# Order of the DMA issues for the score stacks in a Flamingo block on one core: k, then q, then the shift rows, and the low part of q on another engine

## The chip, the cores and the metric

The kernel runs on one core of one Trainium2 chip. The metric is the device time of one execution, in microseconds (us), from first to last instruction with what lies around it. A profiled execution gives a span, first to last instruction of the program, and a time of its own that is slightly longer.

## The reference

Input x is 32 batches of 256 rows by 256 columns in f32, and a context of the same shape. The block is gated cross attention followed by a gated feed-forward network with fake quantisation:

```python
# attention: 16 heads of 16, rotary tables on q and k, band |i-j| <= 50
q = rope(layernorm(x) @ Wq.T + bq)
k = rope(ctx @ Wk.T + bk)
v = ctx @ Wv.T + bv
p = softmax(where(band, q @ k.T / 4, -1e9))
x = x + tanh(g_xattn) * ((p @ v) @ Wo.T + bo)
# feed-forward: weights to 4 bits in blocks of 32, activations to 16 bits
h = act_qdq(layernorm(x))
up, gate = act_qdq(h @ qdq(w_up).T), act_qdq(h @ qdq(w_gate).T)
g = act_qdq(gate * qdq16(sigmoid(gate)))
x = x + tanh(g_ffn) * (act_qdq(g * up) @ qdq(w_down).T)
```

## The kernel before

The program has three stages: the weights are prepared (to about 50 us), attention runs over the 32 batches (to about 840 us), and the feed-forward stage follows. The change touches the attention stage alone.

Attention is a software pipeline written out by hand. Each engine has one instruction queue and runs the same loop `steps(rnd, unit)`, one round per batch, cut into eight slots. In the round of batch b0 the engines also work on the batches before it: b1 is one round older, b2 two, b3 three, b4 four; `nxt` is one younger. Synchronisation is by semaphores, so an engine that waits for one value holds up everything behind it on its queue. TensorE is PE, VectorE is DVE, ScalarE is ACT, GpSimd is POOL, SyncE is SP. SP issues every DMA.

The scores need more precision than bf16 gives, so q and k are each split into three bf16 parts. For n in q, k: POOL adds the two products of the rotation (`rotate`), ACT rounds it to the high part (`high`), DVE subtracts (`remainder`), ACT rounds the rest to the middle part (`middle`), and one more subtraction makes the low part (`low`). For k, `low` is on DVE at the head of slot 5. For q, it is on POOL at the end of slot 5, after that slot's `cut`. SP then stores the parts to DRAM (`store_parts`, 384 KB) and loads them back into a stack of 96 rows, `k_stack` or `q_stack`, in three DMAs of 384, 256 and 128 KB (`load_stacks`). The load waits until the store has landed. There are three buffers of each stack.

PE multiplies the stacks twice. `scores` (L835, S_FIRST = 11: pair 0 of batch b1 in slot 3, a round after its parts were made) gives q by k; PE waits there for both stacks. DVE takes the row maxima out of it (`maxima`, L707). The negated maxima are the shift: DVE splits them (`shift_parts`, L720 and L722), PE transposes them, ACT copies them to `shiftT` (L608), and SP writes them in four small DMAs as rows 96 and 97 of `q_stack` (`load_shift`, L471), half 0 for heads 0 to 7 and half 1 for heads 8 to 15. `scoresT` (L852, ST_FIRST = 18: pair 0 of batch b2 in slot 2) gives k by q with the shift inside the product, and waits on the shift rows of that half. ACT takes exponents of it (L596), POOL cuts the band (L527, L536), and PE weighs V (L878).

In one round SP goes through: shift rows half 0 of b2, load of the q stack of b1, x and context of the next batch, the store and the reload for the residual, shift rows half 1 of b2, store of k of b0, store of q of b0, load of the k stack of b0. Its round begins, in time, when the engines are at slots 0 and 1 of theirs.

Of the kernel before, what the change touches and what calls it, by code (L numbers as in the profile page):

```python
# [12 lines left out]
ALU = mybir.AluOpType  # L13
# [60 lines left out]
def reached(eng, sem, batch, per, k):  # L74

    value = batch.n * per + k
    if value <= 0:
        return
    eng.wait_ge(sem, value)
# [229 lines left out]
def attention(nc, dram, x, ctx_in, scratch, banks, keep):  # L309

    with ExitStack() as ctx:
# [95 lines left out]

            return (slot - first) % SLOTS, (first + (slot - first) % SLOTS) // SLOTS

        def low(eng, by, b, n):  # L410

            if not b.real:
                return
            reached(eng, mid_ready[n], b, 1, 1)
            by.tensor_tensor(parts[n][:, 2, :], rest[n][:], parts[n][:, 1, :], ALU.subtract)\
                .then_inc(low_ready[n], 1)

        S_FIRST, ST_FIRST, PV_FIRST = 11, 18, 20
        block = ctx.enter_context(nc.Block())

        @block.sync
        def _(sp):
            def load_x(b):
                if not b.real:
                    return

                reached(sp, x_transposed, b.before(1), 1, 1)
                sp.dma_start(x_in[:], rows_x[b.n]).then_inc(x_loaded, 16)
                reached(sp, c_transposed, b.before(1), 1, 1)
                sp.dma_start(c_in[:], rows_c[b.n]).then_inc(c_loaded, 16)  # L430

            def load_residual(b):
                if not b.real:
                    return

                bb = b.before(NBUF)
                if bb.n >= 0:
                    sp.wait_ge(x2_stored[b.buf], bb.rnd * 16 + 16)
                reached(sp, x2_normed, bb, T, T)
                sp.dma_start(x2[b.buf][:], rows_x[b.n]).then_inc(xres_loaded[b.buf], 16)  # L440

            def store_parts(b, n):
                if not b.real:
                    return

                reached(sp, mid_ready[n], b, 1, 1)
                reached(sp, low_ready[n], b, 1, 1)

                if b.n >= NBUF:
                    sp.wait_ge(stack_loaded[n][b.buf], b.rnd * 48)  # L450
                sp.dma_start(scratch[n][b.buf].rearrange("k (a d) (h t) -> (d h) (k a) t", a=2, h=H),
                             parts[n][:].rearrange("p k (a t) -> p (k a) t", a=2)).then_inc(parts_stored[n], 16)

            def load_stacks(b, n):
                if not b.real:
                    return
                stack = (q_stack if n == "q" else k_stack)[b.buf]
                reached(sp, parts_stored[n], b, 16, 16)
                reached(sp, scoredT, b.before(NBUF), 2 * PAIRS, 2 * PAIRS)
                row = 0  # L460
                for g in range(3):
                    rows = (3 - g) * DK
                    sp.dma_start(stack[row:row + rows, :, :].rearrange("r s t -> r (s t)"), scratch[n + "_rows"](b.buf, g)).then_inc(stack_loaded[n][b.buf], 16)
                    row += rows

            def load_shift(b, half):
                if not b.real:
                    return
                reached(sp, shiftT_copied, b, HALVES, half + 1)
                for k in range(SHIFT):  # L470
                    sp.dma_start(q_stack[b.buf][STACK + k:STACK + k + 1, half * 8:half * 8 + 8, :],  # L471
                                 shiftT[half][k * 8:(k + 1) * 8, :]).then_inc(shift_loaded[half][b.buf], 16)

            def store_x2(b):
                if not b.real:
                    return
                reached(sp, x2_ready, b, 1, 1)
                sp.dma_start(scratch["x2"][b.n], x2[b.buf][:]).then_inc(x2_stored[b.buf], 16)

            def steps(rnd, unit):  # L480
                load_shift(Batch(rnd, unit, 2), 0)
                load_stacks(Batch(rnd, unit, 1), "q")
                load_x(Batch(rnd, unit, -1))
                store_x2(Batch(rnd, unit, 4))
                load_residual(Batch(rnd, unit, 3))
                load_shift(Batch(rnd, unit, 2), 1)
                store_parts(Batch(rnd, unit, 0), "k")
                store_parts(Batch(rnd, unit, 0), "q")
                load_stacks(Batch(rnd, unit, 0), "k")

            run(steps)
            for k in range(NBUF):
                sp.wait_ge(x2_stored[k], 16 * len(range(k, B, NBUF)))

        @block.gpsimd
        def _(pool):
# [43 lines left out]
            def steps(rnd, unit):  # L540
                for slot in range(SLOTS):
                    if slot == 5:
                        scale_of(Batch(rnd, unit, -1), moments_taken, scale_steps, scale_ready, moments, scale_small, scale)
                    if slot == 2:
                        rotate(Batch(rnd, unit, 0), "k")
                    if slot == 3:
                        rotate(Batch(rnd, unit, 0), "q")
                    if slot == 1:
                        scale_of(Batch(rnd, unit, 4), moments2_taken, scale2_steps, scale2_ready, moments2, scale2_small, scale2)
                    pair, late = pair_at(slot, ST_FIRST)  # L550
                    cut(Batch(rnd, unit, late), pair)
                    if slot == 5:
                        low(pool, nc.gpsimd, Batch(rnd, unit, 0), "q")

            run(steps)
            nc.gpsimd.partition_all_reduce(keep["peak"][:, 6:7], keep["lnconst"][:, 0:1], P, RMAX).then_inc(pool_ready, 1)
# [105 lines left out]
        def _(dve):  # L662
# [27 lines left out]
            def remainder(b, n):  # L690
                if not b.real:
                    return
                reached(dve, high_ready[n], b, 1, 1)

                nc.vector.tensor_tensor(rest[n][:], rot[n][:], parts[n][:, 0, :], ALU.subtract)\
                    .then_inc(rest_ready[n], 1)

            def maxima(b, pair):
# [3 lines left out]
                for t in range(T):  # L702
# [6 lines left out]
                            scale=1.0, scalar=-3e38, op0=ALU.add, op1=ALU.max, accum_out=smax[b.buf][:, t, h:h + 1])  # L709
                    ins.then_inc(max_taken, 1)  # L710

            def shift_parts(b, half):

                if not b.real:
                    return
                reached(dve, max_taken, b, 2 * PAIRS, PAIRS * (half + 1))

                reached(dve, shift_transposed, b.before(1), HALVES, half + 1)
                src = smax[b.buf][:, :, half * 8:half * 8 + 8]
                nc.vector.tensor_copy(shift[:, :, half, 0, :], src).then_inc(shift_high, 1)  # L720
                reached(dve, shift_high, b, HALVES, half + 1)
                nc.vector.tensor_tensor(shift[:, :, half, 1, :], src, shift[:, :, half, 0, :], ALU.subtract)\  # L722
                    .then_inc(shift_ready, 1)
# [31 lines left out]
            def steps(rnd, unit):  # L755
                nxt, b0, b1, b2, b3, b4 = (Batch(rnd, unit, k) for k in range(-1, 5))
                for slot in range(SLOTS):
                    if slot == 0:
                        residual(b4)
                    if slot == 1 and 0 <= b0.n < NBUF:  # L760

                        nc.vector.memset(k_stack[b0.n][STACK:P, :, :], 1.0).then_inc(ones_rows_set, 1)
                    if slot == 2:
                        rope(b0, "k", bank_b)
                        divide(b3, 0)
                    if slot == 3:
                        shift_parts(b2, 1)
                        rope(b0, "q", bank_a)
                    if slot == 4:
                        remainder(b0, "k")  # L770
                    if slot == 5:
                        low(dve, nc.vector, b0, "k")
                        remainder(b0, "q")
                    if slot == 7:
                        shift_parts(b1, 0)
                    pair, late = pair_at(slot, S_FIRST)
                    maxima(Batch(rnd, unit, late), pair)
                    if slot == 5:
                        divide(b3, 1)
                    if slot == 4 and nxt.real:  # L780
                        reached(dve, x_loaded, nxt, 16, 16)
                        statistics(nxt, x_in, stats, moments, stats_taken, moments_taken)
                    if slot == 7 and b4.real:
                        reached(dve, xn2T_copied, b4, 1, 1)
                        nc.vector.tensor_reduce(keep["xmax"][:, b4.n:b4.n + 1], keep["xnT"][:, :, b4.n * S:(b4.n + 1) * S],
                                                XY, ALU.max, apply_absolute_value=True).then_inc(xmax_taken, 1)
# [934 lines left out]
```

## Time and profile before

| | |
|---|---|
| Runs | 1406.34, 1407.23, 1412.29 us, median 1407.23 |
| Profiled execution, its own time | 1405.53 us |
| Its span | 1403.8 us |
| Mean granted TensorE clock | 0.941 |
| Busy over the span | PE 85%, DVE 86%, ACT 60%, POOL 42% |
| DMA queue of SP | 132,250 packets, 205.86 MB |

Busy shares are averages over three stages. What the change touches must be read inside the attention stage, in one round and from the waits there.

### The profile page before, as it was taken

To read this page: it belongs to the slowest core of one execution; us is meant where nothing else is said; L and a number is where in the kernel's file an instruction comes from. 1 tells how busy PE (TensorE), PEld (TensorE's weight loads), DVE (VectorE), ACT (ScalarE), POOL (GpSimd) and SP (SyncE) were. 2 spreads that over 40 slices of the span, in tenths; PEclk is the share of its full clock that TensorE was granted. 3 is DMA by queue.
4 is the path that set the end of the run, shared out by engine and by line. 5 is a ranking of instruction groups with operands and counts; after the bars stand their busy time and mean duration, and the time that the engine had idled before them with its cause. 6 is when DMAs were issued, how large, how long until landed. Compare 5 with 4: busy or idle time off the path is not lost. (4 is left out here: it accounts for less than half of the span.)

```text
span 1403.8 us, 27833 instructions
## 1 busy us (share of the span) xinstructions
PE 1195.9 (85%) x8960; PEld 807.6 (58%) x8992; DVE 1202.3 (86%) x3570; ACT 837.5 (60%) x1336; POOL 587.1 (42%) x1392
## 2 busy tenths in 40 slices
PE   3367898988888888888888767999899979977998
PEld 2245676776766766666676543444333334436887
DVE  5678998999999899899989736998899989997886
ACT  2225665656666565657565545664676779993332
POOL 1127787778778787778777640000000000000000
PEclk7679999999999999999999988999999999998999
DMA  3174856566666667575757311222455455556774
GB/s 113 34 161 108 180 137 159 137 159 148 149 157 149 153 144 158 138 158 139 169 127 170 85 38 45 112 91 111 151 188 187 170 179 193 188 179 203 234 237 164
DMA packets 132369, 207.27 MB, mean 148 GB/s; under 512 B 11159, under 2 KB 97050, under 8 KB 126106
## 3 DMA queue, kind: packets, MB, share of 16 engines
q1 hardware_dynamic: 132250, 205.86, 53.6%
q8 instruction: 53, 0.87, 0.3%
q14 instruction: 66, 0.54, 0.1%
HBM read 125.60 MB, written 79.69 MB: 146 GB/s over the span
## 5 line engine op out<-in xcount | busy, mean ns | idle before, releaser
L596 ACT ACTIVATE probs<-psum 128x356 f32<-128x356 f32 x512 | 210.2, 464 | 246.4 <-PE psum L852 246.4
L707 DVE CUSTOM_DVE_ANT_0 psum<-psum,band 128x178 f32<-128x178 f32 x1024 | 317.2, 372 | 40.1 <-PE psum L835 38.5
L1014 PE MATMUL psum<-xnT,w_upT 128*128 (+1 forms) x1152 | 260.8, 384 | 19.1 <-DVE maxima L1238 8.8
L527 POOL TENSOR_SCALAR_AFFINE_SELECT probs<-probs 128x154 f32<-128x154 f32 (+1 forms) x512 | 214.3, 426 | 146.9 <-ACT probs L596 141.0
L835 PE MATMUL psum<-k_stack,q_stack 96*128 96x178 bf16 x1024 | 143.2, 251 | 88.0 <-issue 57.2
L1014 PEld LDWEIGHTS psum<-xnT,w_upT 128*128 128x128 f16 x1152 | 109.7, 99 | 170.0 <-issue 32.2
L536 POOL TENSOR_SCALAR_AFFINE_SELECT probs<-probs 128x254 f32<-128x254 f32 (+1 forms) x512 | 189.1, 393 | 0.0
L835 PEld LDWEIGHTS psum<-k_stack,q_stack 96*128 96x128 bf16 x1024 | 76.5, 100 | 145.4 <-issue 86.6
L707 DVE DVE_READ_ACCUMULATOR2_ANT smax<- 128x1 f32 x1024 | 142.7, 139 | 0.0
L1614 PE MATMUL psum<-w_downT,xnT 128*128 128x256 f16 x1152 | 128.1, 275 | 16.0 <-DVE xnT L1564 16.0
L1014 PE MATMUL psum<-xnT,w_gateT 128*128 (+1 forms) x576 | 125.9, 382 | 8.7 <-DVE xnT L1087 8.7
L1614 PEld LDWEIGHTS psum<-w_downT,xnT 128*128 128x128 f16 x1152 | 113.8, 99 | 30.6 <-DVE xnT L1564 16.5
L852 PE MATMUL psum<-q_stack,k_stack 98*128 98x178 bf16 x1024 | 126.7, 247 | 2.5 <-DMA q_stack<-shiftT 1.2
L878 PE MATMUL psum<-probs,V 128*32 128x178 f32 x2048 | 113.0, 334 | 1.9 <-POOL probs L536 1.7
L1014 PEld LDWEIGHTS psum<-xnT,w_gateT 128*128 128x128 f16 x576 | 56.6, 98 | 77.9 <-DVE xnT L1087 9.1
L852 PEld LDWEIGHTS psum<-q_stack,k_stack 98*128 98x128 bf16 x1024 | 90.1, 100 | 13.5 <-issue 1.5
L1589 ACT ACTIVATE xnT<-xnT 128x1536 f16<-128x1536 int16 x32 | 47.5, 1484 | 80.7 <-DVE xnT L1545 80.7
L878 PEld LDWEIGHTS psum<-probs,V 128*32 128x32 f32 x2048 | 66.7, 113 | 13.6 <-POOL probs L536 2.1
L1275 ACT ACTIVATE sig<-inner_int,scales 128x1536 f32<-128x1536 int16 x32 | 50.5, 1577 | 40.3 <-DVE maxima L1244 40.2
L810 PE MATMUL psum<-WoT,attT 128*128 128x256 f32 x256 | 62.1, 387 | 7.9 <-ACT attT L567 5.5
L810 PE MATMUL psum<-WvT,cT 128*128 128x256 f32 x256 | 68.1, 413 | 0.0
L819 PE MATMUL psum<-cT,WkT 128*128 128x256 f32 x256 | 65.6, 402 | 0.0
(189 smaller groups left out, 2283.7 us busy)
## 6 DMA issues: line engine op xcount, KB each, us to landing
k_parts_scratch<-k_parts SPq DMA_DIRECT2D x32, 384.0 KB, 2.6
q_parts_scratch<-q_parts SPq DMA_DIRECT2D x32, 384.0 KB, 2.6
k_stack<-k_parts_scratch SPq DMA_DIRECT2D x32, 384.0 KB, 5.1
q_stack<-q_parts_scratch SPq DMA_DIRECT2D x32, 384.0 KB, 6.0
gate_scratch<-g_stage SPq DMA_DIRECT2D x16, 768.0 KB, 3.3
g_in<-gate_scratch SPq DMA_DIRECT2D x16, 768.0 KB, 4.6
sig_scratch<-w_gateT SPq DMA_DIRECT2D x32, 384.0 KB, 2.3
sig_again<-sig_scratch SPq DMA_DIRECT2D x32, 384.0 KB, 3.4
```

The costliest lines, as they stand in the source:

```text
L527: nc.gpsimd.affine_select(out=t[:, :, 0:n], in_=t[:, :, 0:n], pattern=[[0, 2], [1, n]], compare_op=ALU.is_ge, fill=0.0, base=WINDOW - off, ...
L536: nc.gpsimd.affine_select(out=t[:, :, n:SPAN], in_=t[:, :, n:SPAN], pattern=[[0, 2], [-1, SPAN - n]], compare_op=ALU.is_ge, fill=0.0, base ...
L596: nc.scalar.activation(ring_tile(probs, b, pair, c)[:].rearrange("p e j -> p (e j)"), scoreT_bank[c][:, 0:2 * SPAN], ACT.Exp, scale=DK ** ...
L707: ins = nc.vector.tensor_tensor_reduce(out=mine, in0=mine, in1=keep["band"][:, t, :], scale=1.0, scalar=-3e38, op0=ALU.add, op1=ALU.max, a ...
L810: last = nc.tensor.matmul(out, srcT[:, c, t * P:(t + 1) * P], weight[:, c * D:(c + 1) * D], start=(c == 0 and not biased), stop=(c == C - ...
L819: last = nc.tensor.matmul(bank[:, half * S:(half + 1) * S], weight[:, c * D + half * P:c * D + (half + 1) * P], srcT[:, c, :], start=(c == ...
L835: last = nc.tensor.matmul(bank[:, e * SPAN:(e + 1) * SPAN], q_stack[b.buf][0:STACK, h, t * P:(t + 1) * P], k_stack[b.buf][0:STACK, h, t * ...
L852: last = nc.tensor.matmul(scoreT_bank[c][:, e * SPAN:(e + 1) * SPAN], k_stack[b.buf][0:STACK + SHIFT, h, c * P:(c + 1) * P], q_stack[b.buf ...
L878: last = nc.tensor.matmul(out_bank[half][row:row + OUT, col + c * FAR:col + c * FAR + SPAN], V[b.buf][:, v_at:v_at + OUT], ring_tile(probs ...
L1014: last = nc.tensor.matmul(bank[:], weights[wp][:, c * I + f * P:c * I + (f + 1) * P], x_parts[:, c, bass.ds(j * (2 * TILE) + xp * TILE, TI ...
L1275: nc.scalar.activation(sig[h][:], kept(j, h), ACT.Sigmoid, scale=col(G_S)).then_inc(sig_done, 1)
L1614: last = nc.tensor.matmul(bank[:, 0:D], o[odd][f // HF][op][:, at:at + P], keep["w_downT"][wp][:, f * D:(f + 1) * D], start=(f == 0 and k ...
```

## The change

SP's round is reordered. The k stack is loaded directly behind k's store, ahead of q's store. The q stack is loaded directly behind q's store, at the end of the round, where it was at the head of the next one behind the shift rows of half 0. Those shift rows come last. Batch(rnd, unit, 1) at the end of a round and Batch(rnd, unit, 2) at the head of the next are the same batch. The low part of q moves from POOL, end of slot 5, to DVE, head of slot 6. No operation is added or dropped; the `low` subtraction of q changes its engine.

```diff
-        def low(eng, by, b, n):
-            if not b.real:
-                return
-            reached(eng, mid_ready[n], b, 1, 1)
-            by.tensor_tensor(parts[n][:, 2, :], rest[n][:], parts[n][:, 1, :], ALU.subtract)\
-                .then_inc(low_ready[n], 1)
...
@@ block.sync
             def steps(rnd, unit):
-                load_shift(Batch(rnd, unit, 2), 0)
-                load_stacks(Batch(rnd, unit, 1), "q")
                 load_x(Batch(rnd, unit, -1))
                 store_x2(Batch(rnd, unit, 4))
                 load_residual(Batch(rnd, unit, 3))
                 load_shift(Batch(rnd, unit, 2), 1)
-                store_parts(Batch(rnd, unit, 0), "k")
-                store_parts(Batch(rnd, unit, 0), "q")
-                load_stacks(Batch(rnd, unit, 0), "k")
+                for n in "kq":
+                    store_parts(Batch(rnd, unit, 0), n)
+                    load_stacks(Batch(rnd, unit, 0), n)
+                load_shift(Batch(rnd, unit, 1), 0)
@@ block.gpsimd
                     cut(Batch(rnd, unit, late), pair)
-                    if slot == 5:
-                        low(pool, nc.gpsimd, Batch(rnd, unit, 0), "q")
@@ block.vector
+            def low(b, n):
+                if not b.real:
+                    return
+                reached(dve, mid_ready[n], b, 1, 1)
+                nc.vector.tensor_tensor(parts[n][:, 2, :], rest[n][:], parts[n][:, 1, :], ALU.subtract)\
+                    .then_inc(low_ready[n], 1)
...
                     if slot == 5:
-                        low(dve, nc.vector, b0, "k")
+                        low(b0, "k")
                         remainder(b0, "q")
+                    if slot == 6:
+                        low(b0, "q")
```

## Rows read from the trace of the kernel before

**Rows 1.** Waits, 125 to 790 us: engine line waited for, us in total, times, longest.
```profile
PE psum L835 <- issue: 52.9, 29, 3.1
```

**Rows 2.** Timeline of SP, 516 to 542 us: start, us, what it issued.
```profile
522.26 0.37 SPq L451 DMA_DIRECT2D k_parts_scratch<-k_parts  x1
527.38 0.37 SPq L451 DMA_DIRECT2D q_parts_scratch<-q_parts  x1
527.85 1.87 SPq L463 DMA_DIRECT2D k_stack<-k_parts_scratch  x3
529.76 1.39 SPq L471 DMA_DIRECT2D q_stack<-shiftT  x2
531.25 2.71 SPq L463 DMA_DIRECT2D q_stack<-q_parts_scratch  x3
534.00 0.42 SPq L428 DMA_DIRECT2D x_in<-in_x  x1
```

**Rows 3.** Timeline of PE in that round: start, us, in brackets the idle time before.
```profile
517.27 0.47 PE L835 MATMUL psum<-k_stack,q_stack 96*128 96x178 bf16 x4 [1.31 <-issue]
517.58 0.47 PE L852 MATMUL psum<-q_stack,k_stack 98*128 98x178 bf16 x4
...
537.64 0.47 PE L852 MATMUL psum<-q_stack,k_stack 98*128 98x178 bf16 x4
540.09 0.47 PE L835 MATMUL psum<-k_stack,q_stack 96*128 96x178 bf16 x4 [1.98 <-issue]
```

**Rows 4.** Issues and landings, 517 to 529.5 us: KB each, us from issue to landing.
```profile
q_parts_scratch<-q_parts SPq DMA_DIRECT2D x1, 384.0 KB, 2.6
```

**Rows 5.** The same view, 531 to 535.8 us.
```profile
x_in<-in_x SPq DMA_DIRECT2D x1, 256.0 KB, 6.5
c_in<-in_ctx SPq DMA_DIRECT2D x1, 256.0 KB, 6.7
...
q_stack<-q_parts_scratch SPq DMA_DIRECT2D x1, 128.0 KB, 6.6
```

**Rows 6.** The same view, 45 to 62 us, with nothing else in the queue.
```profile
x_in<-in_x SPq DMA_DIRECT2D x2, 256.0 KB, 2.8
```

**Rows 7.** Busy by engine in each stretch; last columns: PE clock, DMA share, GB/s.
```profile
527.00:528.00 1.00, 1.00 (x6) 0.90 (x5) 1.00 (x6) 0.18 (x1) 1.00 (x4) 1.00 0.00 0
528.00:529.00 1.00, 1.00 (x16) 0.71 (x17) 1.00 (x5) 0.36 (x1) 0.60 (x2) 1.00 0.75 229
```

**Rows 8.** Timeline of DVE: k's low part, and the two halves' L722.
```profile
521.53 0.66 DVE L415 TENSOR_TENSOR k_parts<-k_sin,k_parts 128x512 bf16<-128x512 f32 x1
...
526.32 1.03 DVE L722 TENSOR_TENSOR shift<-smax,shift 128x16 bf16<-128x16 f32 x1
...
537.99 0.18 DVE L722 TENSOR_TENSOR shift<-smax,shift 128x16 bf16<-128x16 f32 x1
...
540.44 0.35 DVE L707 CUSTOM_DVE_ANT_0 psum<-psum,band 128x178 f32<-128x178 f32 x1 [0.71 <-PE psum L835]
```

**Rows 9.** Timeline of POOL, 516 to 541 us: q's low part.
```profile
526.16 1.16 POOL L415 TENSOR_TENSOR q_parts<-q_sin,q_parts 128x512 bf16<-128x512 f32 x1
```

**Rows 10.** Instructions on q_parts: ns min/median/max, first and last start.
```profile
L415 POOL TENSOR_TENSOR q_parts<-q_sin,q_parts x32: 1150/1154/1162, 70.4 to 779.5; 128x512 bf16<-128x512 f32 x32
```

**Rows 11.** The 3 us after a batch's first scores, columns as in Rows 7.
```profile
173.40:176.40 3.00, 3.00 (x38) 2.47 (x39) 3.00 (x15) 2.28 (x6) 3.00 (x6) 1.00 0.72 242
...
470.60:473.60 3.00, 3.00 (x28) 2.00 (x29) 1.99 (x9) 1.14 (x4) 2.42 (x5) 0.52 0.48 170
...
771.60:774.60 3.00, 2.99 (x38) 2.47 (x39) 2.64 (x14) 2.31 (x6) 3.00 (x6) 1.00 0.07 21
```

**Rows 12.** Timeline of DVE in the second of those stretches.
```profile
473.85 0.35 DVE L707 CUSTOM_DVE_ANT_0 psum<-psum,band 128x178 f32<-128x178 f32 x1 [0.84 <-PE psum L835]
```

**Rows 13.** Timeline of ACT, 516 to 541 us: the high part of k.
```profile
538.71 0.63 ACT L581 ACTIVATE k_parts<-k_cos 128x512 bf16<-128x512 f32 x1
```

**Rows 14.** Timeline of PE in the first round, 83 to 85 us.
```profile
83.88 0.75 PE L835 MATMUL psum<-k_stack,q_stack 96*128 96x178 bf16 x4 [4.66 <-DMA q_stack<-q_parts_scratch]
```

## The prediction

> **What bounds the kernel now.** I read the page, then the waits in the middle of attention, then one round engine by engine, and last the landings of that round's DMAs.
>
> By the page DVE is the fullest engine, 86% of the span. What is left of it is what a change of order could give back, so the waits matter. From 125 to 790 us PE sits idle 52.9 us in 29 waits before L835, the scores, and the releaser is only called "issue" [rows 1]. The number 29 gives it away: one wait a round, before pair 0, where PE waits on both stacks. The round that I take as the pattern runs from 517.27 to 540.09 us, which is 22.82 us [rows 3]; the mean over the loop is (779.5 - 70.4) / 31 = 22.87 us [rows 10]. In it the last of the three q loads is issued near 533.4 and takes 6.6 us, so it lands at 540.0 [rows 2, 5]. PE starts at 540.09 [rows 3], and DVE, which had waited 0.71 us, at 540.44 [rows 8]. So the period of the loop is a chain that passes through the q stack, with DVE close behind it.
>
> Counted from the first scores (time 0 = 517.27), the chain is: k's store issued at 5.0, q's store at 10.1, q's load at 14.0, all of it landed at 22.7, next scores at 22.82 [rows 2, 3]. The reader should see two more things. The ring of SP is empty before q's store: its DMA share is 0.00 in the microsecond from 527 and 0.75 in the next [rows 7], so data flow about 0.9 us after an issue at 527.38. And the q load is issued 1.3 us after q's store landed (527.38 + 2.6 = 529.98), because SP is busy with the shift rows until 531.15 [rows 2, 4].
>
> **Prices of the transfers.** A transfer's landing depends on what is in front of it. The x load of 256 KB lands after 2.8 us on an empty ring [rows 6] and after 6.5 us behind the q load [rows 5]. In that stream the context load goes out directly behind it, some 0.45 us later (SP takes 0.42 for the x load [rows 2]), and needs 0.2 us longer, so another 256 KB costs 0.7 us of data time [rows 5]. The lone x load then splits into 0.9 start, 0.7 data and 1.2 receipt. A store of 384 KB takes 2.6 [rows 4]; its data time is between 1.0 (by that rate) and 1.7 (2.6 less the start), and I take 1.2. From q's store at 527.38 to the last q landing at 540.0 are 12.6 us, in which the ring never runs dry: start 0.9, store 1.2, two stack loads, receipt 1.2. So a stack load of 768 KB is (12.6 - 3.3) / 2 = 4.65 us of data, and 6.75 us from issue to landing when alone.
>
> **The change, part by part.**
>
> *The k load moves ahead of q's store.* k's store lands at 5.0 + 2.6 = 7.6, and the k load is issued at 7.7 instead of 10.6. SP takes 1.9 us for its three issues [rows 2], so q's store goes out at 9.6 at the earliest. It went out at 10.1 before. But now 768 KB stand in front of it on the ring. It lands at 7.7 + 0.9 + 4.65 + 1.2 + 1.2 = 15.65, not 2.6 us after its issue.
>
> The Trainium skill, "DMA: Bandwidth & Descriptors", section "Queues, rings and completion order", says that each engine takes a ring's descriptors in order and that a semaphore increment lands only after the earlier writes of that engine. By that rule q's store can't be seen as landed before the k load's data are written; the 2.8 against 6.5 us of the x load agree. Without it q's store would land near 12.2, the second rival below.
>
> *The q load follows q's store at once.* Issued at 15.75 (was 14.0), on a ring that has run empty, since SP had to wait. It lands at 15.75 + 6.75 = 22.5. Before it landed at 22.7. So the two barriers in a row cost about what is gained by starting 2.9 us earlier and by not waiting for the shift rows' issue.
>
> *The shift rows of half 0 come last.* They were on the ring at 529.76, that is 12.5, and scoresT pair 0 ran at 537.64, that is 20.4, without a wait [rows 2, 3]. Now they are issued from 17.7 on and lie behind the q load: they land with it or up to 0.3 later, I take 22.6. scoresT pair 0 stands ahead of scores pair 0 on PE's queue. So it waits 2.2 us longer than before, and the scores follow it: four matmuls, 0.3 us [rows 3]. Scores start at 22.6 + 0.1 + 0.3 = 23.0 against 22.82: +0.2 us a round. Queued behind the waiting matmul is all of PE; behind that ACT's exponents of pair 0 and, behind these, ACT's high part of k, which before started at 538.71, 1.07 us after scoresT pair 0, and took 0.63 [rows 3, 13]. It will end some 1.3 us after the scores start. The subtraction that waits for it stands behind DVE's four maxima of pair 0, which take longer than that; I hold it just covered.
>
> *x, context and residual* go out about 2 us later, behind the same landings as before, and are first used five microseconds and more after that. Nothing.
>
> *Low part of q on DVE.* DVE gains one instruction of 0.66 us, the price of k's [rows 8]. POOL loses one of 1.16 us [rows 9]. DVE also loses a stall: L722 handles 16 columns and takes 0.18 us in half 1, but 1.03 us in half 0 [rows 8], where it starts at 526.32 beside POOL's subtraction from 526.16 to 527.32 and ends with it [rows 9]. So DVE's own work changes by 0.66 - 0.85 = -0.2 us a round; the bounds are -0.2 and, if a POOL cut blocks the new instruction as L722 is blocked, +0.5. DVE's round without its wait is 22.82 - 0.71 = 22.1; it becomes 21.9, which lies below the chain of 23.0. The result is worth nothing while the chain sets the period. The instruction sits ahead of the maxima of pair 3, and is ready before SP is done with the k load, so the store does not wait on it.
>
> The Trainium skill, "SBUF — State Buffer", section "Who interferes with whom", states that a DVE instruction with two SBUF inputs contends with a GpSimd instruction that reads SBUF, and whoever is first holds the pair to its end. The 1.03 against 0.18 us agree; by it the moved instruction can be held up by a cut, the upper bound just given.
>
> *PE's clock.* In 27 stretches of 3 us after the first scores of a batch (the first, the last and one between are shown), the granted clock is 0.76 or less in 11, down to half (1.2 instead of 2.4 GHz), 1.00 in the others [rows 11]. PE had then waited about 2 us for the stacks. In the stretch at 470.60 DVE waits 0.84 us for the next scores [rows 11, 12]. The wait grows from 1.98 to about 2.4 us, since scoresT no longer falls into it from the front. I guess five more rounds of this kind: 5 x 0.85 = +4 us. Bounds: 0, and all 16 others, +14.
>
> *First round.* The k load is issued at about 71.4, when k's store of that round has landed, then 7.95 + 0.1 + 6.75 gives 86.2 against 83.88 [rows 14]: +2 us.
>
> **Sum.** 31 x 0.2 + 4 + 2 = +12 us on the profiled time of 1405.5, which gives 1417.7; the median of the runs is 1.7 above the profiled execution, so 1419.
>
> **The rivals.**
>
> *The chain comes out shorter.* If the store's data and receipt run beside the tail of the k load (1.2 less) the chain is 21.8, and DVE's 21.9 sets the period: 31 x 0.9 = 28 less, at most. With half of it, -0.4 a round, 1405.5 + 2 - 12 + 1.7 = 1397. This is the case on the other side. It decides from 0.2 us a round on, that is if the two waits for landings cost less than 14.5 us together (I have 7.95 + 6.75 = 14.7). For it speaks that the two orders are so close, against it the x load.
>
> *q's store isn't held by the k load.* It would land at 9.6 + 2.6 = 12.2, the q load would follow at 12.3, and everything would have landed at 7.7 + 12.6 = 20.3. DVE sets the period at 21.9: -0.9 a round, 1381. The x load speaks against it.
>
> *The chain comes out longer.* If each of the barriers costs 0.5 us more, because the slowest of 16 engines ends them, the period is 24.0: 31 x 1.2 = 37, with all rounds at the low clock +14, +2: 1460. With half of it: 1434.
>
> *Nothing changes.* The two chains come out within 0.1 us, and the clock with them: 1407 to 1412.
>
> **Chances.** The forecast case (1410 to 1428) 0.42; longer (above 1428) 0.16; no change by balance 0.15; shorter chain 0.22; q's store not held 0.05. A change below 0.5%, 7 us, can't be told from none in this kernel. Above 1414: most of the first and all of the second, 0.50. Below 1400: 0.26. Between: 0.24. The range has to hold both signs: 1392 to 1440. The likeliest case's own is 1410 to 1428.
>
> **What would show it.** SP's timeline after: k load some 7.7 us after the scores, q's store 1.9 later, q's load 6 us after the store and not 2.7. q's store: 5.5 to 6.5 us to landing, the q load 5.4 to 5.9 for its 128 KB (less than 6.6, since nothing is ahead). PE's wait moves from L835 to L852, and is then charged to the shift rows or to the q stack. L722 all at 0.18, the L415 row of q on DVE at 0.66 to 1.1. More rows with a clock below 1.00 after the scores. The prediction is wrong if q's store lands within 4 us, if DVE's wait before L707 vanishes, or if the order delays something I hold covered: the high part of k, or x.

## The result, and the profile after

The changed kernel takes 1450.97 us (median of 4 runs, 1447.34 to 1455.24), 1.0301 times the kernel before (95% interval 1.0264 to 1.0338). That is slower, as forecast, but by 43 us where +12 was forecast, and outside the range. The profiled execution took 1451.52 us, its span is 1449.8. Lines of the changed kernel stand 2 to 11 lines higher: L835 is now L833, L852 is L850, L707 is L696, L463 is L455.

The loss is nearly all in the attention stage. The mean period of a round goes from 22.96 to 24.28 us (27 rounds, first scores of a batch to first scores of the next), which is 1.32 us. In the two profiled executions, whose spans differ by 46 us, the first scores of all come 4.6 us later, the 31 rounds take 39 us longer, and what follows the last round's first scores takes 2 us longer. The timeline of SP of the changed kernel, one round:

```profile
578.05 0.38 SPq L443 DMA_DIRECT2D k_parts_scratch<-k_parts  x1
580.85 1.86 SPq L455 DMA_DIRECT2D k_stack<-k_parts_scratch  x3
582.83 0.37 SPq L443 DMA_DIRECT2D q_parts_scratch<-q_parts  x1
588.51 1.82 SPq L455 DMA_DIRECT2D q_stack<-q_parts_scratch  x3
590.37 1.39 SPq L463 DMA_DIRECT2D q_stack<-shiftT  x2
```

Its issues and landings, 580.5 to 583.3 us, then 588 to 591.8 us (KB each, us from issue to landing):

```profile
q_parts_scratch<-q_parts SPq DMA_DIRECT2D x1, 384.0 KB, 5.7
...
k_stack<-k_parts_scratch SPq DMA_DIRECT2D x1, 128.0 KB, 5.7
...
q_stack<-q_parts_scratch SPq DMA_DIRECT2D x1, 128.0 KB, 5.7
```

q's store lands 5.7 us after its issue, against 2.6 in [rows 4]: it does queue behind the k load. It lands at 588.5, 7.65 us after the k load's issue at 580.85, and the q load goes out in the same instant; its last piece lands 5.7 after an issue 1.2 later, so 6.9 for all of it. What follows on PE, ACT and DVE (start, us; in brackets the idle time before):

```profile
572.43 0.48 PE L850 MATMUL psum<-q_stack,k_stack 98*128 98x178 bf16 x4 [2.22 <-DMA q_stack<-shiftT]
572.75 0.47 PE L833 MATMUL psum<-k_stack,q_stack 96*128 96x178 bf16 x4
573.32 0.68 PE L850 MATMUL psum<-q_stack,k_stack 98*128 98x178 bf16 x4
...
574.81 0.48 PE L833 MATMUL psum<-k_stack,q_stack 96*128 96x178 bf16 x4
```

```profile
572.80 0.82 ACT L585 ACTIVATE probs<-psum 128x356 f32<-128x356 f32 x2 [4.81 <-PE psum L850]
573.51 0.63 ACT L570 ACTIVATE k_parts<-k_cos 128x512 bf16<-128x512 f32 x1
574.03 0.83 ACT L585 ACTIVATE probs<-psum 128x356 f32<-128x356 f32 x2
```

```profile
573.11 0.35 DVE L696 CUSTOM_DVE_ANT_0 psum<-psum,band 128x178 f32<-128x178 f32 x1 [0.97 <-PE psum L833]
...
575.17 0.35 DVE L696 CUSTOM_DVE_ANT_0 psum<-psum,band 128x178 f32<-128x178 f32 x1 [0.17 <-PE psum L833]
...
577.22 0.75 DVE L705 TENSOR_TENSOR k_parts<-k_sin,k_parts 128x512 bf16<-128x512 f32 x1
```

The kernel before, in the round of [rows 3], had the exponents of pair 0 here, ahead of the scores at 540.09, and the maxima of pair 1 without a wait here:

```profile
538.00 0.82 ACT L596 ACTIVATE probs<-psum 128x356 f32<-128x356 f32 x2 [2.42 <-PE psum L852]
...
519.50 0.34 DVE L707 CUSTOM_DVE_ANT_0 psum<-psum,band 128x178 f32<-128x178 f32 x1
```

In [rows 3] PE ran scoresT pair 0 2.4 us ahead of the scores and only then waited. Now it waits 2.22 us in front of scoresT, for the shift rows, and scores follow 0.32 us later. The exponents of pair 0 start with the scores instead of 2 us before them. scoresT pair 1 overwrites the banks that they read, so it starts 0.57 us after the scores (0.31 in [rows 3]). The scores of pair 1 stand behind it and slip, and DVE waits 0.17 us for them. k's store goes out at 578.05, 5.30 us after the scores, against 5.0. This is a round at full clock: the granted clock of the 3 us from 572.80 is 1.00. The waits (engine line waited for, us in total, times, longest), 125 to 820 us:

```profile
PE psum L850 <- DMA q_stack<-shiftT: 59.3, 27, 3.6
DVE psum L696 <- PE psum L833: 52.8, 60, 2.8
```

The 29 waits before the scores [rows 1] have become 27 before scoresT. The 3 us after the first scores, as in [rows 11] (busy us of PE, its weight loads, DVE, ACT and POOL, then PE's granted clock, DMA share and GB/s), first, one between and last of 27:

```profile
181.60:184.60 3.00, 2.87 (x31) 1.52 (x29) 1.89 (x9) 2.28 (x6) 2.36 (x5) 0.68 0.38 133
...
548.30:551.30 3.00, 3.00 (x29) 1.91 (x28) 1.88 (x9) 2.24 (x6) 2.48 (x5) 0.50 0.29 100
...
814.80:817.80 3.00, 3.00 (x30) 1.92 (x29) 1.88 (x9) 2.24 (x6) 2.48 (x5) 0.54 0.03 8
```

The clock is below 0.8 in 19 of 27, against 11 of 27 before. In these 19 k's store goes out 6.00 us after the scores on the mean, in the other 8 5.36.

### The profile page after: what moved, and what is told of

It reads as the page before. It is cut to its first block and busy times, and to the rows that moved or that the text cites. A ratio compares the mean times of both kernels' runs of the same rounds, so it can differ in the third digit from the quotient of the medians.

```text
span 1449.8 us, 27833 instructions
## 1 busy us (share of the span) xinstructions
PE 1222.4 (84%) x8960; PEld 814.5 (56%) x8992; DVE 1212.8 (84%) x3602; ACT 831.8 (57%) x1336; POOL 556.4 (38%) x1360
## 5 line engine op out<-in xcount | busy, mean ns | idle before, releaser
L696 DVE CUSTOM_DVE_ANT_0 psum<-psum,band 128x178 f32<-128x178 f32 x1024 | 318.5, 371 | 73.9 <-PE psum L833 68.4
L518 POOL TENSOR_SCALAR_AFFINE_SELECT probs<-probs 128x154 f32<-128x154 f32 (+1 forms) x512 | 206.2, 412 | 214.4 <-ACT probs L585 209.8
L850 PE MATMUL psum<-q_stack,k_stack 98*128 98x178 bf16 x1024 | 137.7, 256 | 73.1 <-DMA q_stack<-shiftT 65.9
L527 POOL TENSOR_SCALAR_AFFINE_SELECT probs<-probs 128x254 f32<-128x254 f32 (+1 forms) x512 | 198.4, 411 | 0.0
L833 PE MATMUL psum<-k_stack,q_stack 96*128 96x178 bf16 x1024 | 144.6, 255 | 38.2 <-DVE smax L696 30.3
L850 PEld LDWEIGHTS psum<-q_stack,k_stack 98*128 98x128 bf16 x1024 | 87.1, 102 | 104.6 <-DMA q_stack<-shiftT 74.5
L696 DVE DVE_READ_ACCUMULATOR2_ANT smax<- 128x1 f32 x1024 | 141.4, 138 | 0.0
L833 PEld LDWEIGHTS psum<-k_stack,q_stack 96*128 96x128 bf16 x1024 | 82.6, 102 | 91.2 <-DVE smax L696 55.9
L876 PE MATMUL psum<-probs,V 128*32 128x178 f32 x2048 | 118.6, 348 | 1.9 <-POOL probs L527 1.7
```

The source lines that it names most:

```text
L518: nc.gpsimd.affine_select(out=t[:, :, 0:n], in_=t[:, :, 0:n], pattern=[[0, 2], [1, n]], compare_op=ALU.is_ge, fill=0.0, base=WINDOW - off, ...
L527: nc.gpsimd.affine_select(out=t[:, :, n:SPAN], in_=t[:, :, n:SPAN], pattern=[[0, 2], [-1, SPAN - n]], compare_op=ALU.is_ge, fill=0.0, base ...
L696: ins = nc.vector.tensor_tensor_reduce(out=mine, in0=mine, in1=keep["band"][:, t, :], scale=1.0, scalar=-3e38, op0=ALU.add, op1=ALU.max, a ...
L833: last = nc.tensor.matmul(bank[:, e * SPAN:(e + 1) * SPAN], q_stack[b.buf][0:STACK, h, t * P:(t + 1) * P], k_stack[b.buf][0:STACK, h, t * ...
L850: last = nc.tensor.matmul(scoreT_bank[c][:, e * SPAN:(e + 1) * SPAN], k_stack[b.buf][0:STACK + SHIFT, h, c * P:(c + 1) * P], q_stack[b.buf ...
L876: last = nc.tensor.matmul(out_bank[half][row:row + OUT, col + c * FAR:col + c * FAR + SPAN], V[b.buf][:, v_at:v_at + OUT], ring_tile(probs ...
```

## The experiments

All ratios are to the kernel before. Periods and offsets are means over 27 rounds of the profiled execution, from the starts in the timelines. "Low clock" counts the rounds whose 3 us after the first scores have a mean granted clock below 0.8. "k's store" is its issue, counted from the first scores; "scores behind q" is the time from the q load's last landing to the scores.

| kernel | time, us | ratio, 95% interval | period | low clock, of 27 | k's store | scores behind q |
|---|---|---|---|---|---|---|
| before | 1408.14 | 1 | 22.96 | 11 | 5.18 | 0.09 |
| changed | 1450.97 | 1.0301, 1.0264 to 1.0338 | 24.28 | 19 | 5.81 | 0.66 |
| e1_shift_before_q | 1420.51 | 1.0065, 1.0037 to 1.0092 | 23.20 | 9 | 5.28 | 0.09 |
| e2_sp_only | 1447.04 | 1.0274, 1.0225 to 1.0322 | 24.28 | 21 | 5.83 | 0.64 |
| e3_low_only | 1400.03 | 0.9936, 0.9914 to 0.9959 | 22.94 | 0 | 5.53 | 0.09 |
| e4_stores_first | 1404.32 | 0.9953, 0.9932 to 0.9973 | 22.88 | 0 | 6.38 | 0.89 |
| e5_pe_kept_busy | 1463.27 | 1.0373, 1.0328 to 1.0418 | 24.68 | 1 | 5.27 | 1.62 |
| e6_shift_late | 1445.19 | 1.0237, 1.0190 to 1.0284 | 24.25 | 18 | 5.80 | 0.74 |
| e7_before_pe_busy | 1415.28 | 1.0030, 1.0009 to 1.0052 | 23.15 | 0 | 4.88 | 0.68 |
| e8_pe_busy_half | 1429.91 | 1.0163, 1.0119 to 1.0208 | 23.58 | 1 | 5.29 | 0.64 |
| e9_before_pe_busy_half | 1397.51 | 0.9929, 0.9906 to 0.9951 | 22.60 | 0 | 4.90 | 0.09 |
| e10_shift_first_busy | 1413.79 | 1.0018, 0.9997 to 1.0039 | 23.20 | 0 | 4.93 | 0.14 |

The period is also the sum of four stretches, here as means over the same 27 rounds (the last stretch ends at the next batch's scores, so it can differ by 0.03 from the column above). The first two lines are the prediction's own chain.

| kernel | scores to k's store | k's store to q load's issue | q load to landing | landing to scores | period |
|---|---|---|---|---|---|
| predicted, before | 5.0 | 9.0 | 8.7 | 0.1 | 22.8 |
| predicted, changed | 5.0 | 10.75 | 6.75 | 0.5 | 23.0 |
| before | 5.18 | 9.41 | 8.28 | 0.09 | 22.96 |
| changed | 5.81 | 10.65 | 7.18 | 0.64 | 24.28 |
| e6_shift_late | 5.80 | 8.32 | 9.40 | 0.73 | 24.25 |
| e1_shift_before_q | 5.28 | 10.67 | 7.16 | 0.09 | 23.20 |
| e9_before_pe_busy_half | 4.90 | 9.16 | 8.45 | 0.09 | 22.60 |
| e10_shift_first_busy | 4.93 | 10.97 | 7.16 | 0.14 | 23.20 |
| e8_pe_busy_half | 5.29 | 10.61 | 7.06 | 0.61 | 23.58 |

**Shift rows ahead of the q load.** The changed kernel, with the loop over k and q written out and the shift rows moved ahead of the q load.

```diff
-                for n in "kq":
-                    store_parts(Batch(rnd, unit, 0), n)
-                    load_stacks(Batch(rnd, unit, 0), n)
+                store_parts(Batch(rnd, unit, 0), "k")
+                load_stacks(Batch(rnd, unit, 0), "k")
+                store_parts(Batch(rnd, unit, 0), "q")
                 load_shift(Batch(rnd, unit, 1), 0)
+                load_stacks(Batch(rnd, unit, 0), "q")
```

> The changed kernel, but SP issues the shift rows of half 0 between q's store and q's load, while it waits for the store anyway. Theory A (the late shift rows cost more than their own 0.3 us, since scoresT pair 0 and with it ACT and POOL run late, and k's store slips by 0.4 to 0.8 us): the wait before scoresT pair 0 goes, scores start 0.1 us after the q load has landed instead of 0.64, k's store goes out 5.0 to 5.2 us after the scores instead of 5.8, period 24.24 -> about 23.1, time 1412 to 1420. Theory B (the whole loss is that q's store waits behind the k load; the shift rows are hidden behind the q load that PE waits for anyway): the period changes by 0.3 us at most, time 1440 to 1451.

It took 1420.51 us, 30 less than the changed kernel. SP has the time: in its timeline the shift rows go out and the store still has to land.

```profile
564.98 0.37 SPq L443 DMA_DIRECT2D q_parts_scratch<-q_parts  x1
567.47 1.41 SPq L463 DMA_DIRECT2D q_stack<-shiftT  x2
569.93 1.85 SPq L455 DMA_DIRECT2D q_stack<-q_parts_scratch  x3
```

PE in the next round (its lines are L851 and L834) runs scoresT pair 0 early again, and waits in front of the scores:

```profile
575.12 0.47 PE L851 MATMUL psum<-q_stack,k_stack 98*128 98x178 bf16 x4
577.04 0.47 PE L834 MATMUL psum<-k_stack,q_stack 96*128 96x178 bf16 x4 [1.45 <-issue]
```

The period, 23.20 us, and the scores behind the q load, 0.09, came as theory A had them. The time lies 0.5 us above its range, and k's store, 5.28, 0.08 above. Theory B, whose range begins at 1440, falls. So about 30 of the 43 us hang on the position of two transfers of 4 KB each in the queue.

**SP's order alone.**

```diff
 # the kernel before; SP's loop alone is changed:
-                load_shift(Batch(rnd, unit, 2), 0)
-                load_stacks(Batch(rnd, unit, 1), "q")
...
+                for n in "kq":
+                    store_parts(Batch(rnd, unit, 0), n)
+                    load_stacks(Batch(rnd, unit, 0), n)
+                load_shift(Batch(rnd, unit, 1), 0)
```

> SP's new order alone; q's low part stays on GpSimd. Both theories: as the changed kernel, since q's store can't land before the k load, and the low part is ready on GpSimd 10.1 us after the scores where SP has issued the k load at about 10: 1446 to 1456. If the low part on VectorE is what costs, it comes out under 1430.

1447.04 us, inside the range. The intervals of this and of the changed kernel overlap widely. In the new order it makes no difference that can be told which engine makes q's low part.

**The low part alone.**

```diff
 # SP and all else as before
-                    if slot == 5:
-                        low(pool, nc.gpsimd, Batch(rnd, unit, 0), "q")
...
+                    if slot == 6:
+                        low(dve, nc.vector, b0, "q")
```

> The move of q's low part to VectorE alone, SP's order as before. The low part is ready at about 8.2 instead of 10.1 us after the scores, so q's store and the k load start 1.8 us earlier and the ring is through with both loads at about 21 instead of 22.7; the q load itself is still issued behind the shift rows at 13.9. Theory A: VectorE becomes the bound at about 22.0 a round: 31 x -0.8, 1380 to 1392. Rival (VectorE sets the period already, and the move adds 0.66 us to it): 1410 to 1430.

1400.03 us: faster by 0.6%, and in neither range. DVE hardly waits for the scores any more: 3.8 us in all from 125 to 790 us, against 26.6 before. A wait for PE's projection of the attention output (L810) has grown from 0.6 us to 14.4:

```profile
DVE x L747 <- PE psum L810: 14.4, 9, 1.7
DVE psum L705 <- PE psum L835: 3.8, 5, 1.5
```

The clock is low in no round. But DVE's round came out at 22.9 and not at the 22.0 that I had. The stall of the 16-column instruction is gone. Its rows in this kernel (L720) and in the changed one (L718) have 325 and 322 ns as their longest, where the one in [rows 8] took 1.03 us:

```profile
L720 DVE TENSOR_TENSOR shift<-smax,shift x64: 174/236/325, 93.6 to 812.4; 128x16 bf16<-128x16 f32 x64
...
L718 DVE TENSOR_TENSOR shift<-smax,shift x64: 174/177/322, 97.7 to 855.0; 128x16 bf16<-128x16 f32 x64
```

DVE's busy time in the 665 us, though, is more than the 602.40 before, in almost as many rounds:

```profile
125.00:790.00 665.00, 595.41 (x5458) 452.68 (x5456) 611.79 (x2776) 424.44 (x952) 505.94 (x1215) 0.97 0.63 150
```

9.4 us more over 29 rounds is +0.3 us a round, not -0.2. Counted by group of instructions, 0.69 came in with the new one, 0.46 went with L722 and 0.09 with the cast ahead of it, and 0.14 came in with the subtraction behind k's high part (21.7 us before, 25.8 now). The stall of 0.85 was that of one round; the mean, 0.55, is two thirds of it. The pattern round misled in the base too: without its wait it was 22.1 us, and the mean of all rounds, 22.96 less 0.52 of wait, is 22.4. That gives 22.7. The wait that grew, for PE (13.8 us in 29 rounds), is of the size of what is missing, but that it makes the rest is not shown.

**Both stores first.**

```diff
                 for n in "kq":
                     store_parts(Batch(rnd, unit, 0), n)
+                for n in "kq":
                     load_stacks(Batch(rnd, unit, 0), n)
                 load_shift(Batch(rnd, unit, 1), 0)
```

> The changed kernel with both stores ahead of both loads, shift rows last. q's store no longer lies behind the k load: it lands 2.6 us after its issue. All is landed about 21 us after the scores, the shift rows right behind. If the barrier behind the k load is the greater part of the loss, 1390 to 1405. If the late shift rows are the greater part, 1415 to 1430 and the wait of scoresT pair 0 on them stays near 2 us.

1404.32 us, in the range that blamed the barrier, and faster than both kernels. The shift rows are last here too, but everything lands earlier in the round and they no longer hold PE up: PE waits 3.8 us for them in all of 125 to 790 us, in 7 waits.

```profile
PE psum L851 <- DMA q_stack<-shiftT: 3.8, 7, 0.9
```

The loss can so be removed from either side, by moving the rows in e1 or by earlier landings here. The two gains, 30 and 47 us, are together more than the loss of 43, so they don't add. Here, as in the run before, DVE hardly waits for the scores (2.6 us in all), so anything further would be hidden behind its own work. This run alone can't tell the price of the barrier from that of the late rows, since it takes both away.

**Shift rows late in the kernel before.**

```diff
             def steps(rnd, unit):
-                load_shift(Batch(rnd, unit, 2), 0)
                 load_stacks(Batch(rnd, unit, 1), "q")
+                load_shift(Batch(rnd, unit, 2), 0)
```

> The kernel before with one swap: SP issues the q load first and the shift rows of half 0 behind it. q's low part and all else as before. Theory A (late shift rows cost by themselves, through the order scoresT pair 0, exponents, scoresT pair 1): TensorE waits some 2 us before scoresT pair 0, scores start 0.5 to 0.9 us after the q load has landed, k's store slips by 0.3 to 0.8 us, +0.8 to +1.1 us a round, 1433 to 1444. Theory B (they are hidden behind the q load): q's load goes out up to 1.3 us earlier, 1400 to 1412.

1445.19 us, 1 us above theory A's range and far from B's, with one DMA pair moved behind the q load and nothing else. It shows the same picture as the changed kernel: 27 waits before scoresT (125 to 820 us), 18 rounds of 27 with a low clock, k's store at 5.80. By the table of stretches the transfers take as long as before, 8.32 + 9.40 = 17.7 us against 9.41 + 8.28 = 17.7. All of the 1.28 us a round is in k's store (+0.62) and between the q landing and the scores (+0.64).

```profile
PE psum L852 <- DMA q_stack<-shiftT: 66.0, 27, 3.5
```

By the ratios this one swap costs 2.4%, where the whole change costs 3.0%.

**TensorE kept busy.** Matmuls whose result is overwritten are put ahead of PE's wait. In the changed kernel:

```diff
             def scoresT(b, pair):
...
+                if pair == 0:
+                    reached(pe, exp_done, b, 2 * PAIRS, -1)
+                    for _ in range(8):
+                        nc.tensor.matmul(scoreT_bank[0][:, 0:D], keep["WkT"][:, 0:P], keep["WqT"][:, 0:D],
+                                         start=True, stop=True)
                 if pair % 4 == 0:
                     pe.wait_ge(shift_loaded[pair // 4][b.buf], ...)
```

> The changed kernel with eight idle matmuls of 128 x 256 in f32 (0.24 us each at full clock) on TensorE ahead of the wait for the shift rows, into a bank that the next matmul overwrites. Nothing else is changed. Theory A with a share for the clock: the granted clock stays up in the 3 us after the scores (it was below 0.8 in 19 of 27 rounds), k's store goes out 5.3 us after the scores in every round instead of 5.8, and 19 rounds gain about 0.7 us: 1434 to 1442. Rival (the low clock only follows from the longer period and costs nothing): 1447 to 1455. If the late shift rows were clock alone, it would reach 1420.

1463.27 us, slower still and outside every range. The timeline of PE shows that the fault is in my edit.

```profile
576.67 3.62 PE L847 MATMUL psum<-WqT,WkT 128*128 128x256 f32 x16
580.12 0.47 PE L855 MATMUL psum<-q_stack,k_stack 98*128 98x178 bf16 x4
```

The profile counts an f32 matmul of this size twice, so eight are sixteen entries and take 3.62 us, more than the wait they were to fill. The clock and k's store did as expected (1 round of 27 low, 5.27). The same in the kernel before, six ahead of the wait for the stacks:

```diff
             def scores(b, pair):
                 if pair == 0:
+                    reached(pe, max_taken, b, 2 * PAIRS, -1)
+                    for _ in range(6):
+                        nc.tensor.matmul(score_bank[0][:, 0:D], keep["WkT"][:, 0:P], keep["WqT"][:, 0:D],
+                                         start=True, stop=True)
                     pe.wait_ge(stack_loaded["k"][b.buf], b.rnd * 48 + 48)
```

> The kernel before with six idle matmuls of the same kind ahead of the wait for the stacks. It prices the low clock by itself: 11 of 27 rounds ran with it, 0.7 us a round longer than the others. If that is its price, 1398 to 1404; if the transfers set the period whatever the clock, 1406 to 1411.

1415.28 us, above both ranges, with the same fault: scores 0.68 us behind the q load. Both were repeated with half as many matmuls.

```diff
-                    for _ in range(8):
+                    for _ in range(4):
```

> As the run with eight idle matmuls in the changed kernel, with four. An f32 matmul of 128 x 256 took 0.45 us there, not 0.24, so eight held TensorE 3.6 us, longer than the wait of 2.3 us, and scores came 1.62 us after the q load instead of 0.64. Four take 1.85 us and end inside the wait. If the low clock has a share in the loss: low clock in few rounds, k's store at 5.3 after the scores, 0.5 us a round less than the changed kernel, 1433 to 1442. If it has none: 1447 to 1455.

1429.91 us, 21 less than the changed kernel and below what I expected. In the round shown PE is at work until 0.26 us before scoresT, and the clock stays at 1.00 in 26 of the 27 stretches:

```profile
556.08 1.89 PE L847 MATMUL psum<-WqT,WkT 128*128 128x256 f32 x8
558.23 0.48 PE L855 MATMUL psum<-q_stack,k_stack 98*128 98x178 bf16 x4 [0.26 <-DMA q_stack<-shiftT]
```

```profile
558.50:561.50 3.00, 2.87 (x39) 1.99 (x37) 2.43 (x12) 2.91 (x8) 2.35 (x5) 1.00 0.55 193
```

```diff
-                    for _ in range(6):
+                    for _ in range(3):
```

> As the run with six idle matmuls in the kernel before, with three, 1.4 us, inside its wait of 1.9 us. There six delayed the scores to 0.68 us after the q load. If the low clock costs 0.3 us a round on the mean of all rounds (k's store at 4.88 instead of 5.18 after the scores): 1398 to 1404. If the transfers make up for it: 1406 to 1412.

1397.51 us, just below its range and 0.7% faster than the kernel before, by three matmuls for nothing ahead of a wait. It is the lowest median of all, though its interval overlaps those of e3 and e4. All 27 stretches have a clock of 1.00; one of them:

```profile
470.40:473.40 3.00, 3.00 (x38) 2.47 (x39) 2.69 (x16) 2.36 (x6) 2.67 (x5) 1.00 0.41 144
```

**Both remedies.** e1 with the three matmuls of e9.

```diff
 # SP as in e1_shift_before_q
                 if pair == 0:
+                    reached(pe, max_taken, b, 2 * PAIRS, -1)
+                    for _ in range(3):
+                        nc.tensor.matmul(score_bank[0][:, 0:D], ...)
                     pe.wait_ge(stack_loaded["k"][b.buf], b.rnd * 48 + 48)
```

> Both remedies in the changed kernel: the shift rows ahead of the q load, and three idle matmuls ahead of the wait for the stacks. What is left of the change is the k load ahead of q's store and the q load on an empty ring. Against the kernel before with the same three matmuls (1397.5, 22.60 us a round) it prices these alone, at a high clock. Theory: the two orders of the transfers cost the same within 0.3 us a round: 4.9 + 2.64 + 7.95 + 7.15 + 0.15 = 22.8, 1398 to 1408. Rival (the barrier behind the k load is the loss): 1412 or more.

1413.79 us, above what I expected, and just inside the rival's range. Its profiled execution was a long one (1418.7 us), so its period of 23.20 is some 0.15 too high for the median. Against e9 it is 1.0018 - 0.9929 = 0.9% slower at the same clock. That is the price of the order of the four transfers together with q's low part on DVE: some 13 us, 0.4 us a round. e1 against the kernel before gives 0.65% for the same thing, with 9 and 11 rounds at a low clock. From k's store to the q landing this profile has 18.1 us, the others with the new order 17.7 to 17.8, and the old order 17.6 to 17.7, so the price may well be lower than 0.4.

**The loss taken apart.** From before (with its clock held, e9) to changed, in percent of the kernel before: order of transfers and low part +0.9 (e9 to e10), shift rows late at a held clock +1.45 (e10 to e8), and the clock +1.4 in the changed kernel (e8 to changed) against 0.7 before (e9 to before), so +0.7. They add up to 3.0 by the way they are formed, so the sum is no check of them. Each of the three has an interval of some 0.3 to 0.6 either way. They come from different comparisons, and the parts are not independent: e1 takes 2.4 off at once because early shift rows bring the clock back as well (9 low rounds of 27, not 19). What checks them is e6, which puts the late rows and their low clock at 2.4 on an order that is otherwise the old one.

## Why the prediction was wrong

The sign held, and so did the path through the transfers. What failed is the step on the late shift rows: it counted them as 0.2 us a round with everything behind them covered, and it left k's store where it was, 5.0 us after the scores. The sum was +12 us, and 43 were measured; the forecast case's range ended at 1428 and the given range at 1440. In the table of stretches the change adds 1.32 us a round: 0.63 in k's store, where the prediction had nothing, 0.55 between the q landing and the scores, where it had 0.4, and 0.14 in the transfers, where it had -0.2.

*q's store behind the k load.* Right, and closer than the working deserves: 7.95 us from the k load's issue to the landing of q's store predicted, 7.96 measured (mean of 28 rounds; the median is 7.7). The rival in which it isn't held falls. The Trainium skill's rule on ring order and the semaphore that comes behind earlier writes ("DMA: Bandwidth & Descriptors", "Queues, rings and completion order") agrees with the 5.7 us to landing.

*The lone q load.* 6.75 us predicted, 7.17 measured (mean of 28, 7.07 the median): +0.4 us a round. This term was mis-sized. I had divided a busy stretch into start, data and receipt, and the split gave the single load too little. It is of the size that e10 has against e9, and of the 0.34 by which the transfers exceed the predicted change; that it is the whole of either is argued and not shown.

*The shift rows come last.* The step that failed: "they land with it or up to 0.3 later [...] Scores start at 22.6 + 0.1 + 0.3 = 23.0 against 22.82: +0.2 us a round", and behind ACT's high part of k, "I hold it just covered". That part of k was covered: ACT has it done at 574.14, DVE subtracts behind its maxima without a wait. I looked at the one instruction queued behind ACT's exponents and not at the banks they read. scoresT pair 1 waits for them, and behind that the scores of pair 1. At the same clock these come 1.58 us after the first scores in e10 and 2.07 in e8; DVE's maxima of pair 1 start 0.26 us later, its low part of k takes 0.75 us instead of 0.66, and k's store, where the round's chain of transfers begins, goes out 0.36 us later (4.93 in e10, 5.29 in e8). The longer subtraction goes with a band cut on POOL that in e8 starts 0.19 us ahead of it and ends 0.22 us into it; in e10 the cut starts in the same instant as the subtraction. Scores follow the q load by 0.64 instead of 0.14. These two pieces make 0.86 us a round, yet the periods of the two profiled executions differ by 0.38 only, since e10's, a long one, has slower transfers. By the ratios the late rows cost 1.45% at a held clock, 20 us, 0.65 a round. I had priced the step, together with both barriers, at 0.2.

*PE's clock.* "I guess five more rounds of this kind: 5 x 0.85 = +4 us." There were eight more of 27, and nine more of all 32 batches: 23 against 14. Over the 32, the low clock costs 21 us for 20 stretches by e8 (which has 3) against the changed kernel, and 10 us for 13 by e9 (which has 1) against before. That is 0.8 to 1.05 us each, so the price of 0.85 was fair. The change's share is 10 us. That idle time of PE ahead of the scores brings the low clock is shown by the matmuls that fill it; the count was a guess and too small. The length of the wait alone doesn't tell which round it will be: in the changed kernel it is 2.3 us on the mean ahead of the 19 low rounds and 2.2 ahead of the other 8.

*x, context and residual; low part of q.* The first cost nothing that shows. The second is free in the new order (e2). The stall that it was to remove is gone, but DVE's busy time in a round grew by 0.3 in e3 instead of shrinking by 0.2, since the new instruction took 0.69, the subtraction for k 0.14 more, and the stall had been 0.55 on the mean; the floor that I gave the "shorter chain", 21.9, came out at 22.9 in e3 and e4, where DVE hardly waits for the scores, so neither rival on the faster side could have come about at its full price. The contention rule of the Trainium skill ("SBUF — State Buffer", "Who interferes with whom") agrees with 322 ns as the longest, where 1.03 us had been taken beside GpSimd's subtraction.

*First round.* The first scores come at 88.48 us where 86.2 was predicted and 83.88 was measured before: +4.6 us and not +2.

*The longer chain.* Of the rivals the time lies in the range of this one, which had it from slower barriers. The order of the transfers makes 0.4 us a round by e10; the rest came from the shift rows and the clock. So it was not this rival either.

A fault of method lies under several of these: the sum went from one pattern round at full clock, where k's store stood at 5.0 (mean 5.18) and the period at 22.82 (mean 22.96). It had no slow round in it, and the change makes slow rounds.

## What to carry to other kernels

A transfer of a few KB (two of 4 KB here, 2.4% of the time) costs as much as what waits for it. When rows on a shared queue are put behind a large load, look at which wait on the consumer's queue comes first, and follow from there every buffer that is read later than before, not only every instruction.

Where TensorE has a wait in each round, as here, the matmul clock can be part of the price: take it as its own term, with the count of rounds that show it. Three matmuls for nothing ahead of such a wait took 0.7% off this kernel; six, which ended after it, made it 0.3% slower.

## What the runs showed of the hardware that was not expected

The low clock cost 0.8 to 1.05 us for each 3 us stretch that shows it (21 us for 20, 10 us for 13), in a loop where TensorE is not the fullest engine (583.5 us busy against DVE's 602.4 from 125 to 790 us). And the same stores and loads in two orders on one ring end within 0.5 us of each other per round (17.6 to 17.7 us from k's store to the q landing against 17.7 to 18.1), though one order makes the issuing engine wait for a landing twice.
